# A fused image-and-text transformer of two layers: square sums by one matmul per pair, dispatch tails of two groups in one pass, and 64-row matmuls first in every second expert step

## The reference, cut to what matters

```python
# patch embedding: t is [tokens, 3840]
mu = jnp.mean(t, axis=-1, keepdims=True)
var = jnp.mean(jnp.square(t - mu), axis=-1, keepdims=True)
tn = (t - mu) * jax.lax.rsqrt(var + 1e-05) * ln_weight + ln_bias
# experts: g = 8 groups of 192 tokens, 8 experts, 60 slots per expert and group
dispatch = jax.nn.one_hot(prio_se, C, dtype=x.dtype)
expert_in = jnp.einsum('gsec,gsd->egcd', dispatch, xg)
h = jax.nn.relu(jnp.einsum('egcd,edf->egcf', expert_in, wi))
expert_out = jnp.einsum('egcf,efd->egcd', h, wo)
out = jnp.einsum('gsec,egcd->gsd', combine, expert_out)
```

## Time and profile before

| what | value |
|---|---|
| runs before | 405.19, 406.63, 407.81 us; median 406.63 |
| the profiled execution's own time | 405.3 us |
| its span, first to last instruction | 403.2 us |
| mean granted TensorE clock | 0.958 of 2.4 GHz |
| TensorE busy | 377.6 us (94%), 3760 matmul records |
| VectorE, ScalarE, GpSimd busy | 196.0, 113.8, 36.7 us |

### The profile page before, as it was taken

The page is one execution under the profiler, slowest core; times in us unless marked ns, Lnnn a source line. Parts: engine busy times, 40 slices in busy tenths (PEclk is TensorE's granted clock), DMA queues, the critical chain, the costliest instruction groups (busy, mean ns, idle before and its releaser), DMA issues. The chain is left out here.

```text
span 403.2 us, 8731 instructions
## 1 busy us (share of the span) xinstructions
PE 377.6 (94%) x3760; PEld 269.6 (67%) x3760; DVE 196.0 (49%) x550; ACT 113.8 (28%) x220; POOL 36.7 (9%) x76
## 2 busy tenths in 40 slices
PE   4999999999979998999999999999999999897874
PEld 4989877887867532747566474655776766676574
DVE  4857798765944371114223132302153547967653
ACT  1213245565520333231413213031103123232130
POOL 7002230111020010000000000000011111110100
PEclk9998999999995999999999999999999999996868
DMA  7936960000000000031230303000000000000004
GB/s 283 312 80 200 246 147 2 6 4 3 2 3 0 0 2 0 2 117 29 91 89 30 118 2 119 0 2 0 2 2 0 2 2 1 2 2 2 1 0 117
DMA packets 13426, 20.35 MB, mean 50 GB/s; under 512 B 2954, under 2 KB 9580, under 8 KB 13388
## 3 DMA queue, kind: packets, MB, share of 16 engines
q1 hardware_dynamic: 13388, 19.80, 17.0%
HBM read 18.61 MB, written 1.18 MB: 49 GB/s over the span
## 5 line engine op out<-in xcount | busy, mean ns | idle before, releaser
L604 PE MATMUL banks<-sb_wo_sl,sb_attn_hidT_attn 128*60 128x192 f32 x768 | 64.1, 327 | 0.0
L604 PEld LDWEIGHTS banks<-sb_wo_sl,sb_attn_hidT_attn 128*60 128x60 f32 x768 | 52.9, 133 | 10.8 <-issue 2.4
L1059 ACT ACTIVATE sb_attn_hidT_attn<-banks 128x480 f32<-128x480 f32 x48 | 24.8, 568 | 99.9 <-PE banks L590 99.9
L1493 DVE COPY sb_w_tok_e_out<-banks 60x384 f32<-60x384 f32 x32 | 17.8, 555 | 71.5 <-PE banks L604 71.0
L586 PE MATMUL banks<-sb_tok_xeT,sb_wi_sl 128*128 128x480 f32 x96 | 45.1, 592 | 1.1 <-ACT sb_tok_xeT L1051 1.1
L586 PEld LDWEIGHTS banks<-sb_tok_xeT,sb_wi_sl 128*128 128x128 f32 x96 | 16.3, 189 | 25.4 <-issue 23.5
L1483 DVE TENSOR_TENSOR sb_comb<-sb_cst,sb_slot_of 128x480 f32<-128x480 f32 x12 | 7.8, 654 | 39.4 <-PE banks L219 39.4
L414 PE MATMUL banks<-sb_tok_xeT 128*128 128x193 f32 (+1 forms) x128 | 26.0, 353 | 0.0
L590 PE MATMUL banks<-sb_tok_xeT,sb_wi_sl 64*128 64x480 f32 x96 | 25.8, 615 | 0.0
L414 PEld LDWEIGHTS banks<-sb_tok_xeT 128*128 128x128 f32 (+1 forms) x128 | 22.3, 201 | 3.0 <-issue 2.6
L571 PE MATMUL banks<-sb_onehot_combT,sb_xn 64*64 64x480 f32 (+1 forms) x144 | 21.8, 586 | 0.0
(11 more groups left out here) (203 smaller groups left out, 572.0 us busy)
## 6 DMA issues: line engine op xcount, KB each, us to landing
sb_wo_sl<-in_wo SPq DMA_DIRECT2D x8, 576.0 KB, 4.9
sb_tok_xeT<-in_xin SPq DMA_DIRECT2D x8, 448.0 KB, 6.8
sb_wi_sl<-in_wi SPq DMA_DIRECT2D x8, 288.0 KB, 3.2
sb_wi_sl<-in_wi SPq DMA_DIRECT2D x24, 96.0 KB, 3.2
sb_w_tok_e_out<-in_wtok SPq DMA_DIRECT2D x2, 960.0 KB, 6.4
out<-sb_h SPq DMA_DIRECT2D x16, 72.0 KB, 1.8
sb_w_tok_e_out<-in_wtok SPq DMA_DIRECT2D x1, 576.0 KB, 8.6
sb_w_tok_e_out<-in_wtok SPq DMA_DIRECT2D x1, 480.0 KB, 3.6
```

The source lines that it names most:

```text
L604: mm = nc.tensor.matmul(PS[64 * z:64 * z + CAP, 4 + hf, pr * D:(pr + 1) * D], hidT[:, e % 2, f, g * CAP:(g + 1) * CAP], wo_sl[:, q, f], st ...
L1059: nc.scalar.activation(hidT[:, e % 2, f], PS[:, HID_BANKS[(e * (FT // 2) + f // 2) % 2][f % 2], 0:SLOTS], ACT.Relu).then_inc(sem("hidT"), 1)
L1493: ve.tensor_copy(e_out[64 * (e % 2):64 * (e % 2) + CAP, hf * 4 + z:hf * 4 + z + 3:2, e // 2], PS[64 * z:64 * z + CAP, 4 + hf, 0:2 * D].rea ...
```

## The change

1. ScalarE scales each inner pixel by the square root of its count before squaring (`root`, made by GpSimd from `mult` with a power 0.5), tiles 0, 2, 4 by one column and tiles 1, 3, 5 by the other; the two halo tiles are squared together, with the unused rows of tile 7 zeroed once by GpSimd. VectorE folds all eight tiles into one. TensorE sums it with a single matmul against ones.
2. Tails are dispatched for two groups in one pass: group 2p's tail into PSUM rows 0 to 63, group 2p+1's into rows 64 to 127. Each is then copied twice into `xeT`, by ScalarE for hf = 0 and by VectorE for hf = 1. There are six uses of the banks instead of eight.
3. In every second step of an expert (n = 1) the two 64-row matmuls come first and open the accumulation.

```diff
...
+DISP_USE = (0, 1, 3, 5)
+TAIL_USE = (2, 4)
-        x_fold = sb("x_fold", [128, 2, 2, 128])
+        x_fold = sb("x_fold", [128, 2, 128])
+        root = sb("root_mult", [128, 2])
+            then(gp.memset(root_half[:], 0.5))
+            then(gp.memset(x_k[HALO2:128, :, KT - 1], 0.0))
             gp.wait_ge(sem("cst_in"), 16)
+            gp.tensor_tensor(root[:], const("mult")[:, 0:2], root_half[:], ALU.pow).then_inc(sem("root_mult"), 1)
...

             def square_sums(n):
                 pe.wait_ge(sem("x_fold"), n + 1)
-                squares = [(x_fold[:, n % 2, 0], 0, 128), (x_fold[:, n % 2, 1], 1, 128), (x_sq[:, n % 2, KT_IN], KT_IN, 128),
-                           (x_sq[0:HALO2, n % 2, KT - 1], KT - 1, HALO2)]
-                for i, (lhs, t, rows) in enumerate(squares):
-                    mm = nc.tensor.matmul(PS[:, TOK_BANK[n], 200:201], lhs, const("mult")[0:rows, t:t + 1],
-                                          start=(i == 0), stop=(i == len(squares) - 1))
-                mm.then_inc(sem("tok_ps"), 1)
+                nc.tensor.matmul(PS[:, TOK_BANK[n], 200:201], x_fold[:, n % 2], ones[:, 0:1], start=True, stop=True
+                                 ).then_inc(sem("tok_ps"), 1)
...
+            def dispatch(j):
+                use = DISP_USE[j]
+                banks = DISP_BANKS[use % 3]
+                if use < 3:
+                    pe.wait_ge(sem("a_kexp"), GRP * J)
+                    pe.wait_ge(sem("a_vexp"), 4 * J)
+                need(pe, "xeT", (0, 0, 2, 8)[j])
+                need(pe, "xeT_second", (0, 0, 0, 4)[j])
+                for blk in range(NB):
+                    pe.wait_ge(sem("onehot"), NB * j + blk + 1)
+                    for hf in range(2):
+                        rows = slice(64 * hf, 64 * hf + 64)
+                        mm = nc.tensor.matmul(PS[:, banks[hf], 0:E * CAP], xn2[rows, j, blk, 0:128], onehot[rows, j % 2, blk],
+                                              start=(blk == 0), stop=(blk == NB - 1), skip_group_check=True)
+                mm.then_inc(sem("disp_ps"), 1)
+
+            def dispatch_tails(p):
+                use = TAIL_USE[p]
+                banks = DISP_BANKS[use % 3]
+                if p == 0:
+                    pe.wait_ge(sem("a_sub"), J)
+                else:
+                    pe.wait_ge(sem("xeT"), 4)
                 for blk in range(NB):
+                    for z in range(2):
+                        if blk == 0:
+                            pe.wait_ge(sem("onehot"), NB * (2 * p + z) + NB)
                         for hf in range(2):
                             rows = slice(64 * hf, 64 * hf + 64)
+                            mm = nc.tensor.matmul(PS[z * DT:(z + 1) * DT, banks[hf], 0:E * CAP], xn2[rows, 2 * p + z, blk, 128:D],
+                                                  onehot[rows, z, blk], start=(blk == 0), stop=(blk == NB - 1),
                                                   skip_group_check=True)
                 mm.then_inc(sem("disp_ps"), 1)
...
+                    for whole in ((True, False) if n % 2 == 0 else (False, True)):
+                        first = whole == (n % 2 == 0)
+                        for z in range(2):
+                            f = 2 * n + z
+                            rows = slice(z * DT, (z + 1) * DT)
+                            if whole:
+                                lhs, rhs = wi_sl[:, q, f * 128:(f + 1) * 128], xeT[:, 0, e]
+                            else:
+                                lhs, rhs = wi_sl[rows, q, F + n * 128:F + (n + 1) * 128], xeT[rows, 1, e]
+                            mm = nc.tensor.matmul(PS[:, banks[z], 0:SLOTS], lhs, rhs.rearrange("k g c -> k (g c)"),
+                                                  start=first, stop=not first)
+                            if not first:
+                                mm.then_inc(sem("hid_ps"), 1)
...
-            dispatch(0, 0)
+            dispatch(0)
             route_logits(3)
-            dispatch(0, 1)
-            dispatch(1, 0)
+            dispatch(1)
+            dispatch_tails(0)
             count_choices(1)
-            dispatch(1, 1)
-            dispatch(2, 0)
-            dispatch(2, 1)
-            dispatch(3, 0)
-            dispatch(3, 1)
-
-            pe.wait_ge(sem("xeT"), 4 * J)
+            dispatch(2)
+            dispatch_tails(1)
+            dispatch(3)
+
+            pe.wait_ge(sem("xeT"), 16)
+            pe.wait_ge(sem("xeT_second"), 8)
...

-                nc.scalar.activation(x_sq[:, n % 2, 0:KT - 1], x_k[:, n % 4, 0:KT - 1], ACT.Square)
-                nc.scalar.activation(x_sq[0:HALO2, n % 2, KT - 1], x_k[0:HALO2, n % 4, KT - 1], ACT.Square
-                                     ).then_inc(sem("x_sq"), 1)
+                if n == 0:
+                    act.wait_ge(sem("root_mult"), 1)
+                for c in range(2):
+                    nc.scalar.activation(x_sq[:, n % 2, c:KT_IN:2], x_k[:, n % 4, c:KT_IN:2], ACT.Square, scale=root[:, c:c + 1])
+                nc.scalar.activation(x_sq[:, n % 2, KT_IN:], x_k[:, n % 4, KT_IN:], ACT.Square).then_inc(sem("x_sq"), 1)
...
+            def keep_tails(p):
+                act.wait_ge(sem("disp_ps"), TAIL_USE[p] + 1)
+                for z in range(2):
+                    src = dispatched(DISP_BANKS[TAIL_USE[p] % 3][0], slice(z * DT, (z + 1) * DT))
+                    for copy in range(2):
+                        nc.scalar.copy(xeT[copy * DT:(copy + 1) * DT, 1, :, 4 * p + 2 * z], src).then_inc(sem("xeT"), 1)
...
+            keep_dispatched(1)
+            keep_tails(0)
+            keep_dispatched(2)
+            keep_tails(1)
+            keep_dispatched(3)
...

-                ve.tensor_reduce(x_fold[:, n % 2], x_sq[:, n % 2, 0:KT_IN].rearrange("k (t c) n -> k c n t", c=2), AX_X, ALU.add
+                ve.tensor_reduce(x_fold[:, n % 2], x_sq[:, n % 2].rearrange("k t n -> k n t"), AX_X, ALU.add
                                  ).then_inc(sem("x_fold"), 1)
...
-                need(ve, "disp_ps", 2 * (j - 1))
+                need(ve, "disp_ps", (0, 0, 3, 3)[j])
...
+            def keep_tails(p):
+                ve.wait_ge(sem("disp_ps"), TAIL_USE[p] + 1)
+                for z in range(2):
+                    src = PS[z * DT:(z + 1) * DT, DISP_BANKS[TAIL_USE[p] % 3][1], 0:E * CAP].rearrange("k (e c) -> k e c", e=E)
+                    for copy in range(2):
+                        ve.tensor_copy(xeT[copy * DT:(copy + 1) * DT, 1, :, 4 * p + 2 * z + 1], src
+                                       ).then_inc(sem("xeT_second"), 1)
...
             mark_slots(0)
             mark_slots(1)
             choose(1)
+            keep_tails(0)
             gates(1)
             place(1)
             mark_slots(2)
             mark_slots(3)
+            keep_tails(1)
             slot_norms()
```

More of the change, by code:

```diff
@@ L562, in dispatch @@
+            def dispatch_tails(p):
+                use = TAIL_USE[p]
+                banks = DISP_BANKS[use % 3]
+                if p == 0:
                     pe.wait_ge(sem("a_sub"), J)
+                else:
+                    pe.wait_ge(sem("xeT"), 4)
                 for blk in range(NB):
-                    if part == 0:
-                        pe.wait_ge(sem("onehot"), NB * j + blk + 1)
-                    for z in range(1 + part):
-                        cols = slice(128, D) if part else slice(0, 128)
-                        outs = slice(z * DT, (z + 1) * DT) if part else slice(0, 128)
+                    for z in range(2):
+                        if blk == 0:
+                            pe.wait_ge(sem("onehot"), NB * (2 * p + z) + NB)
@@ L569, in dispatch @@
                         for hf in range(2):
                             rows = slice(64 * hf, 64 * hf + 64)
-                            mm = nc.tensor.matmul(PS[outs, banks[hf], 0:E * CAP], xn2[rows, j, blk, cols],
-                                                  onehot[rows, j % 2, blk], start=(blk == 0), stop=(blk == NB - 1),
+                            mm = nc.tensor.matmul(PS[z * DT:(z + 1) * DT, banks[hf], 0:E * CAP], xn2[rows, 2 * p + z, blk, 128:D],
+                                                  onehot[rows, z, blk], start=(blk == 0), stop=(blk == NB - 1),
```

34 lines of the change are left out of this document (7 added, 27 removed).

## The result

| kernel | median of 7 runs | profiled execution: own time, span, mean granted clock |
|---|---|---|
| before | 406.63 us (404.97 to 408.35) | 405.3, 403.2, 0.958 |
| after | 402.04 us (399.93 to 403.93) | 400.5, 398.6, 0.957 |

Ratio 0.9887, 95% interval 0.9844 to 0.9929: the change gives 4.6 us. The forecast was 7.9 us (398.7, range 395.0 to 402.5). The direction held, and the range by 0.5 us; the median lies just outside the forecast's own range (396.8 to 401.6), and 3.3 us of the gain are missing. (Each ratio here leaves out executions over 1.5% above the fastest of their kernel; in the experiments that cuts up to 16 of 29 runs of before, so medians of all runs stand beside the ratios there.)

What follows compares the result with a forecast made beforehand. TensorE, busy 94% of the span, was taken as the bound, with VectorE next in the square-sum stage. Parts of 3.5, 1.4 and 3.0 summed to 7.9 us: 406.63 to 398.7, own range 396.8 to 401.6, wider range 395.0 to 402.5.

Steps and rivals of the forecast that it cites:

- Part 3, forecast 3.0: Experts: six blocks become four per expert, saving two edges of 0.19 us, eight times: 3.0 us; bounds 3.0 and 0.6.
- Rival C: Experts: merged blocks pay for their weight loads, part 3 gives only 0.6 us, total 401.1 us; chance 0.08.
- Part 2, forecast 1.4: Dispatch: experts start 2.4 us earlier, less 1.0 for a clock fall after a new stall; bounds 5.1 and -2.7.
- minus 1.0 for the clock: Dispatch: the new 2.5 us stall brings a short low-clock stretch, losing 0.75 to 1.7 us, taken as 1.0.
- Part 1, forecast 3.5: Square sums: TensorE sheds 6.4 us, but VectorE becomes the stage's bound, leaving 3.5 us; bounds 6.4 and 2.0.
- The lower bound of 2.0: Part 1's least gain, if the low clock falls into a stretch where VectorE's slack is used up.
- The prediction's "chain": VectorE's work from pair 2's to pair 6's statistics, 18.97 us becoming 18.95; pair 6 ready and value matmuls starting at 53.95.
- Rival A: Whole kernel: stalls cost nothing, VectorE is quick enough or the clock stays up; 392.1 us at most; chance 0.15.
- B: Rival: stalls eat more; part 1 2.0, part 2 -2.7 by a long low stretch, part 3 3.0; 404.3 us; chance 0.12.
- D: Rival: slower than before; TensorE's pauses at each pair keep 1.2 GHz from 35 to 61 us; 410.7 us; chance 0.02.

Runs made afterwards that it cites:

- tails and order: Kernel after with before's squares, fold and sums, so only the new dispatch and expert order; median 403.0 us (12 runs), ratio 1.0005 to before.
- squares alone: Kernel before with only the square sums changed (part 1); median 404.05 us (12 runs), ratio 0.9993 to before.
- gates_first: Kernel after with VectorE's second-round gates moved ahead of its copies of the first tails; median 401.28 us (10 runs), ratio 0.994 to before.
- gates_first_old: Kernel after with the gates ahead of the tail copies and the square sums of before; median 401.52 us (12 runs), ratio 0.9964 to before.

## Why the prediction was right, and where its sum was off

**Part 3, forecast 3.0, measured 3.18: right.** Two edges (changes between 128-row and 64-row blocks) fewer in each expert gave 8.43 - 8.04 us, 0.20 for an edge, where 0.19 was read from the earlier trace rows. Rival C (merged blocks pay for their loads, 0.6) is out. The Trainium skill, "TensorE: Matmul & The Clock Gate", section The mechanism, says that a weight load overlaps running matmuls only when the row group differs. This case's trace does not agree: a merged block loads the same rows again, and each edge saved gave the full 0.20 us, where the prediction's estimate by the page was 0.08. Here the measurement decides.

**Part 2, forecast 1.4: the waits and copies right, the clock wrong.** The wait came where it was put and as large (2.81 for 2.5 us), the four copies took 2.71 for 2.6, the block after the wait ended at 146.24 for 146.5. Without the clock 2.4 was forecast, and at equal low clock 2.29 was measured. The clock did fall behind the wait, and cost 4.38 - 2.69 = 1.7 us of the block, the upper end of what I named. But "minus 1.0 for the clock" took before's profile for its normal state. The old dispatch has the same 3.4 us low in two of the kernels that kept it. Against before's profiled 16.95 the part shows 0.59, against 18.65 it shows 2.29. And the prediction looked for the clock's price behind the new wait only. Over whole runs the kernels with the new dispatch have some 9 us more low time (0.954 in after for 0.965), and in the medians the part shows no gain: -2.3 alone, -0.5 on top of part 3.

**Part 1, forecast 3.5: the term that failed.** "With a fixed part of about 0.2 us it is 1.30": I carried the fold's price over by elements from sums of three to sums of eight, and it was 1.92. That is 0.62 us more for each of eight folds on the engine which the prediction itself had named the bound of this stage. The prediction also counted four folds from pair 2's to pair 6's statistics, 1.1 us; there are three, of pairs 4 to 6, and at 0.89 each they add 2.7 us. By the timeline pair 6's statistics end 34.7 us after the first patches; the forecast had 53.95 - 21.76 = 32.2. Of the 2.5 us, 1.1 were lost before pair 2's statistics (35.40, 14.4 after the first patches, for 13.2) and 1.4 from there to pair 6 (20.4 for 18.95). The value matmuls started 55.91 - 21.03 = 34.9 us after the first patches, before 57.31 - 21.76 = 35.6: 0.7 us, where 3.4 was forecast. Before has a pause in those matmuls, which makes them 3.05 us long (57.31 to 60.36) for after's 2.25, and its sum of pair 7 is heavier; these raise the gain to 1.57 by queries 2, and the first of them is not the prediction's mechanism. The pause, in the timeline of before:

```profile
59.90 0.53 PE L469 MATMUL banks<-sb_w_v,sb_xrT 97*32 97x96 f32 x13 [0.44 <-issue]
```

My own mark of failure, a fold over 1.6 us, was the right one. The lower bound of 2.0 allowed for the clock and not for this price.

**What the stretch behind gave back.** Of the 1.57 us 1.46 went between queries 2 and 4, where nothing was changed. Two pauses of TensorE are 1.0 of it by their idle time. By starts, the two blocks that hold them take 0.90 and 0.64 us longer than in before, which is all of it. After's timeline:

```profile
72.99 0.66 PE L472 MATMUL banks<-sb_w_v,sb_xrT 97*32 97x96 f32 x18 [0.65 <-issue]
...
84.17 0.40 PE L488 MATMUL banks<-sb_attn_hidT_attn,sb_qT 32*32 32x96 f32 x15 [0.37 <-issue]
```

These are of the same kind as the 2.55 above, and each of the fourteen kernels has one to three of them before 110 us, at other places (tails and order 0.75, 1.38 and 0.35). The prediction's "chain" ended at the value matmuls, and what came after was counted as shifted whole. How much of part 1 is lost to them in the median can't be told: 1.4 us by squares alone, 1.0 by after against tails and order, 0.2 by gates_first against gates_first_old, all within the scatter.

**Sum.** At like clock the parts are 0.1 (first patches to queries 4: 74.87 to 74.75), 2.3 and 3.2: 5.6 us, less what the clock makes of the rest; measured 4.6. But the 0.1 is one pair of kernels. Tails and order and after differ by part 1 alone too, with 3.4 us of low clock each, and there it is 76.91 - 74.75 = 2.2 us, since tails and order has the longer pauses. So the missing 3.3 us have two sources that these runs show and cannot divide: part 1, 0.1 to 2.2 us in the profiled executions (2.9 under the new order of gates) where 3.5 was forecast, by the fold's price and by pauses that no term of the sum had; and the lower clock of the kernels with the new dispatch, up to 5 us against the 28 us of low time in before's 29 runs, where the sum had 1.0. Rival A (stalls cost nothing) was wrong by the waits of 2.15 and 2.81 us. B was half right: the stalls ate more, but part 1 by the fold's price, and part 2, by the medians, by low clock elsewhere, with no long low stretch in the dispatch. D did not come: first patches to queries 2 has one low stretch of 3.4 us, as before.

**The signs on record, and luck.** These came: TensorE waits for VectorE after pair 2, it stands still 2.81 us before the third group's block, the clock falls in the dispatch, one expert is 0.39 us shorter. These did not: the value matmuls start at 55.91 and not near 54, the fold is over 1.6 us, and the experts start 2.91 us earlier (152.63 for 155.54), less than the 3.5 named as a sign of being wrong, and 0.73 of that is the earlier start of the first patches. So the forecast was wrong in part 1 and right in its total only by a wide range: 402.04 is within 402.5, a bound that was set for rival C, which did not come, and for the scatter. The single runs of after went up to 403.93.

## What to carry to other kernels

Price a reduction by how many distant elements go into one sum, and measure the new shape before trading matmuls for it, above all when the engine that takes it over is the next bound. Work that needs nothing from a wait belongs in front of it: moving five small operations took 1.2 us from a wait of 2.8 (the medians do not resolve what the kernel gained). When the clock's low stretches shift by several us from one execution to the next, compare stretches at equal low time over many kernels; neither one profile's span nor its lucky stretch is a baseline. And look at the mean clock of every run: a part can win its own stretch and lose it elsewhere, as the new dispatch did.
